# Node sums with the one-hots stationary and the messages in two exact halves, in a graph layer on one Trainium2 core

## The chip, the cores and the metric

One core of a Trainium2 chip runs the whole program. The metric is the device time of one execution in microseconds (us), lower is better. The kernel before takes 1014.85 us, the median of three executions (1013.4 to 1015.24). Engine names: PE is TensorE, ACT ScalarE, DVE VectorE, POOL GpSimd, SP SyncE, which here only issues DMAs.

## What is computed

The layer has three parts over 3125 nodes of 256 numbers and 50000 edges that are sorted by their target. The graph part is the one the change touches:

```
xn  = layernorm(x)
e   = edge_attr @ W_edge + b_edge            # 50000 x 256
msg = relu(xn[src] + e)
agg = segment_sum(msg, dst)                  # 3125 x 256, f32
h   = (1 + eps) * xn + agg
h   = relu(h @ W1 + b1) @ W2 + b2            # then a batch norm over nodes and a relu
x   = x + relu(bn(h)) + linear_attention(xn)
x   = x + mixture_of_experts(layernorm(x))   # 8 experts, top 2, 1024 hidden
```

## The kernel before

All engine programs are written out by hand, with semaphores between them. There are four stages: norms and tables (to about 50 us of the profile), the **edge stage** (to about 560 us), the two-layer MLP with batch norm and the routing (to about 670 us), and the expert blocks (to the end).

The edge stage takes the edges in 66 groups of 768, six tiles of 128 edges each; the last group has one tile. Every engine runs its own loop over n, the number of the group, one group behind the other. For a group:

- SP loads the edge attributes (`load_edges`, L428). POOL gathers the 256 numbers of each edge's source node from a table in HBM, one indirect DMA for each tile of 128 edges (L775), that is 391 in all. They go to a ring of six buffers of two tiles, so POOL may run 12 gathers ahead of DVE's use; each gather reads its row numbers from the table `srcT` in SBUF.
- PE turns the six tiles of attributes (L439), ACT copies them to SBUF (`eaT`, L484), and PE multiplies them by `w_edge` (the embedding, `embed_edges`, L450) into three PSUM banks.
- DVE adds the gathered nodes, pair of tiles by pair (`add_nodes`, L526), into `msg`, and ACT applies the relu in place (`relu_messages`, L498).
- DVE makes the one-hots of the targets inside a window of 128 nodes (`mark_window`, L502, or `mark_from_psum`, L508, which reads its counting row from PSUM). PE multiplies messages and one-hots in full f32 (`aggregate`, L476): the message tile, 128 edges by 128 of the 256 columns, is the stationary operand, the one-hot (128 edges by 128 nodes) the moving one. The sums come out with the columns on the partitions, as the node array `hT` is kept, and DVE adds them to `hT` at the group's window (`add_window`, L544).

Work of other parts rides in the same loops. For n up to 50: keys, values and queries of the attention (PE L924, L932, L941; ACT L1248 to L1250, L1257, L1258; DVE `mix_h` L1571, `mix_k` L1584, `mix_q` L1589). For n from 51: the attention's denominators and outputs (PE L972, L983; ACT L1274, L1280; DVE reciprocals L1604, two for each group, and L1610, one for every two). In every group the expert weights are split in two exact halves for later use: ACT rounds a piece (`round_high`, L581, to the type fp32r), DVE subtracts (`round_low`, L587), SP stores both (L574, L575).

The order in each loop is the order of the code. DVE in iteration n: `mix_h`, `add_window(n - 2)`, the one-hots, `mix_k`, a reciprocal, the three node sums, `mix_q`, `round_low`, a reciprocal and L1610. ACT: the copy of group n + 1's turned attributes, attention work, the three relus of group n, `round_high`. PE: the turn of group n + 1, the embedding of group n, `aggregate(n - 1)`, attention work. After the last group DVE's memset L1697 raises `edges_done`, on which the MLP starts (PE L1040). The input `x`, overwritten by its norm early on, is loaded again into `xs` during n = 51 to 55 (L661), and needed first in front of L1745.

Of the kernel before, what the change touches and what calls it, by code (L numbers as in the profile page):

```python
# [21 lines left out]
F32 = mybir.dt.float32  # L22
# [75 lines left out]
def build(nc, a, out):  # L98
    with ExitStack() as ctx:
# [17 lines left out]
        qT = sb("qT", [P, HALVES, NODES_PAD])  # L117
        xs = sb("xs", [P, TILES, DIM])
# [20 lines left out]
        onehot = view(work, 7680, 2, GT, P)  # L139
# [168 lines left out]
        msg_ready = sem("msg_ready")  # L308
# [150 lines left out]
        def aggregate_tail(pe, n, u):  # L459
            pe.wait_ge(agg_read, n)  # L460
            pe.wait_ge(onehot_ready, n + 1)
            pe.wait_ge(msg_ready, PAIRS * (n + 1))
            for h in range(HALVES):
                last = nc.tensor.matmul(bank[5][:, h * P:(h + 1) * P], msg[:, u, 0, h * P:(h + 1) * P], onehot[:, u, 0],
                                        start=True, stop=True)
            last.then_inc(agg_ready, 1)

        def aggregate(pe, n, u, fresh=False):
# [9 lines left out]
            last.then_inc(agg_ready, 1)  # L478
# [12 lines left out]
        def relu_tail(act, n, u):  # L491
            act.wait_ge(sums_done, PAIRS * (n + 1))
            nc.scalar.activation(msg[:, u, 0], msg[:, u, 0], ACT.Relu).then_inc(msg_ready, PAIRS)
# [27 lines left out]
        def add_nodes(dve, n, u):  # L521
            for q in range(PAIRS):
# [15 lines left out]
        def add_window(dve, n, start, mixed, fresh=False):  # L538
            dve.wait_ge(agg_ready, n + 1)
# [4 lines left out]
            nc.vector.tensor_tensor(w, bank[5][:, 0:DIM].rearrange("p (h c) -> p h c", h=HALVES),  # L544
# [60 lines left out]
        def _(sp):  # L605
# [44 lines left out]
            for n in range(2, GROUPS - 1):  # L650
# [8 lines left out]
                c = n - 2 * TILES - 1  # L659
                if 0 <= c < CHUNKS:  # L660
                    for d, s in node_rows(a["x"], xs[:, c * CHUNK_TILES:(c + 1) * CHUNK_TILES], c):  # L661
                        sp.dma_start(s, d).then_inc(x_again, 16)
# [17 lines left out]
            sp.wait_ge(edges_done, 1)  # L680

# [168 lines left out]
        def _(pe):  # L850
# [140 lines left out]
            for n in range(GROUPS):  # L991
                if n + 1 < GROUPS:
                    transpose_group(n + 1)
                if n < GROUPS - 1:
                    embed_edges(pe, n, n % 2, n == 0)
                else:
                    embed_tail(pe, n, n % 2)
# [5 lines left out]
                if n >= 1:  # L1003
                    aggregate(pe, n - 1, (n - 1) % 2, n == 1)
# [12 lines left out]
            aggregate_tail(pe, GROUPS - 1, (GROUPS - 1) % 2)  # L1017
            again = pe.value_load(miss_i[0:1, 0:1], min_val=0, max_val=1)
            with pe.If(again > 0):
# [5 lines left out]
                with pe.Fori(0, WINDOWS) as w:  # L1025
                    with pe.Fori(0, GROUPS) as g:
# [3 lines left out]
                        aggregate(pe, n, 0)  # L1030
            with pe.Else():
# [169 lines left out]
        def _(act):  # L1201
# [89 lines left out]
            nc.scalar.copy(xw[:], bank[7][0:XROWS, 0:SPLIT * TILE]).then_inc(xw_copied, 1)  # L1291
            for n in range(GROUPS):
                if n + 1 < GROUPS:
                    copy_group(n + 1)
                if 1 <= n <= 2 * TILES:
                    if n % 2 == 1:
                        mix_kv(n // 2)
                    else:
                        mix_q(n // 2 - 1)
                if n == DEN0:  # L1300
# [5 lines left out]
                if n < GROUPS - 1:  # L1306
                    relu_messages(act, n, n % 2)
                else:
                    relu_tail(act, n, n % 2)
# [10 lines left out]
                if n == 6:  # L1320
                    nc.scalar.copy(w2_hi[:], w2[:]).then_inc(w12_high, 1)
            again = act.value_load(miss_i[0:1, 0:1], min_val=0, max_val=1)
            with act.If(again > 0):
                with act.Fori(0, WINDOWS) as w:
                    with act.Fori(0, GROUPS) as g:
                        n = (w + 1) * GROUPS + g
                        copy_edges(act, n, 0, False, 1)
                        relu_messages(act, n, 0)
# [150 lines left out]
        def _(dve):  # L1479
# [140 lines left out]
            for n in range(GROUPS):  # L1620
# [3 lines left out]
                if n >= 2:  # L1624
                    add_window(dve, n - 2, starts[(n - 2) % GT], mixed_by(n + 1), n == 2)
# [9 lines left out]
                if n % 2 == 1 and n < 2 * TILES:  # L1635
                    mix_k(n // 2)
                if n == 2 * TILES:
                    mask_context()
                c, late = (n - DEN0 - 1) // 2, (n - DEN0 - 1) % 2
                if 0 <= c < COL_CHUNKS and not last:  # L1640
                    attn_inverse(c, 2 * late)
                if last:
                    add_tail(dve, n, n % 2)
                else:
                    add_nodes(dve, n, n % 2)
                if n % 2 == 0 and 2 <= n <= 2 * TILES:
# [19 lines left out]
            with dve.If(again > 0):  # L1666
# [16 lines left out]
                with dve.Fori(0, WINDOWS) as w:  # L1683
                    dve.wait_ge(pass_done, w + 1)
                    dve.sem_inc(pass_begun, 1)
                    with dve.Fori(0, GROUPS) as g:
                        n = (w + 1) * GROUPS + g
                        mark_window(dve, g, 0)
                        add_nodes_again(dve, n)
                        add_window(dve, n, w * WINDOW, TILES)  # L1690
# [280 lines left out]
```

## Time and profile before

| | |
|---|---|
| median of three executions | 1014.85 us |
| the profiled execution, its own time | 1009.37 us |
| its span (first to last instruction) | 1007.6 us |
| PE busy | 926.4 us, 92% |
| DVE busy | 601.8 us, 60% |
| POOL busy | 544.6 us, 54% |
| ACT busy | 538.3 us, 53% |
| mean granted TensorE clock | 0.967 of full |

A group row of the profile reads: line, engine, operation, output<-input, shape and count | busy us, mean ns of one | idle us of the engine just before them <- what ended that idle time. "issue" is time in which the engine waited for nothing that the profile shows. In the timeline, each row is the start in us, the duration, the engine, the line, the operation, and in brackets the idle time before it. SBUF tensors that were cut out of larger ones are printed by the larger one's name: `work` holds the messages, one-hots, gathered rows and attributes, `wts` the pieces of weights and `qn`.

### The profile page before, as it was taken

How to read it: one execution, taken by the hardware profiler on the slowest of the kernel's cores; microseconds unless marked ns; L12 is line 12 of the kernel's file. 1: busy time of each engine (PE TensorE's matmuls, PEld its weight loads, DVE VectorE, ACT ScalarE, POOL GpSimd, SP SyncE). 2: the span in 40 equal slices, each digit the busy share in tenths (PEclk: the TensorE clock that was granted, in tenths of full speed). 3: DMA queues.
4: the chain of work that ended last, by engine and by line, in shares of the span. 5: the costliest groups of instructions: out<-in, count | busy, mean ns of one | idle time of the engine just before them, and what ended most of it. 6: DMA issues, size and time to landing. Idle time of an engine off the chain costs nothing.

```text
span 1007.6 us, 17432 instructions
## 1 busy us (share of the span) xinstructions
PE 926.4 (92%) x6055; PEld 824.6 (82%) x6055; DVE 601.8 (60%) x1098; ACT 538.3 (53%) x1064; POOL 544.6 (54%) x527
## 2 busy tenths in 40 slices
PE   5899999999999999999999975379999999999995
PEld 4677889889888888897888765368999999999994
DVE  5555665565665565568989778835554454555442
ACT  2744545445545455445545564836555666555552
POOL 3277777777777777777774004023444444444433
PEclk8899999999999999999999998589999999999998
DMA  9667888877878878799775105459799789888722
GB/s 247 198 165 231 264 259 266 254 253 251 277 243 260 274 252 262 249 304 324 248 241 184 43 1 182 168 201 384 236 312 308 239 289 301 279 253 301 244 42 28
DMA packets 93173, 234.59 MB, mean 233 GB/s; under 512 B 20425, under 2 KB 37843, under 8 KB 84122
## 3 DMA queue, kind: packets, MB, share of 16 engines
q1 hardware_dynamic: 56694, 116.95, 33.9%
q0 software_dynamic: 29136, 64.72, 26.5%
q10 hardware_dynamic: 7252, 51.75, 12.8%
q8 instruction: 52, 0.85, 0.3%
q14 instruction: 39, 0.32, 0.1%
HBM read 183.81 MB, written 50.23 MB: 232 GB/s over the span
## 4 chain that ended last, share of the span: by engine, by line
PE 59%; POOL 13%; DMA 10%; DVE 8%; issue 7%; ACT 2%; DVEq 0%; POOLq 0%; SPq 0%; ACTq 0%
PE banks L1154 15%; POOL work L775 13%; PE banks L1174 10%; DMA work<-node_table,srcT 8%; PE banks L476 7%; PE banks L450 7%; PE banks L1176 5%; PE banks L924 3%; PE banks L983 2%; PE banks L439 2%; PE banks L1063 2%; PE banks L1051 1%; DVE work L526 1%; PE banks L1138 1%; DMA wts<-in_src 1%
## 5 line engine op out<-in xcount | busy, mean ns | idle before, releaser
L775 POOL DMA_INDIRECT work<-node_table,srcT x391 | 382.9, 979 | 151.6 <-issue 109.8
L498 ACT ACTIVATE work<-work 128x512 f32<-128x512 f32 x195 | 120.9, 630 | 127.0 <-DVE work L526 126.3
L476 PEld LDWEIGHTS banks<-work 128*128 128x128 f32 x1560 | 184.2, 192 | 4.5 <-DVE hT L544 1.1
L476 PE MATMUL banks<-work 128*128 128x128 f32 x1560 | 184.8, 275 | 0.7 <-DVE hT L544 0.7
L450 PE MATMUL banks<-w_edge,eaT 128*128 128x256 f32 x780 | 179.1, 379 | 0.0
L526 DVE TENSOR_TENSOR work<-banks,work 128x512 f32<-128x512 f32 x195 | 128.0, 682 | 69.5 <-DMA work<-node_table,srcT 55.1
L824 POOL DMA_INDIRECT out<-work,row_i x54 | 86.5, 1601 | 141.5 <-ACT work L1444 118.9
L1154 PE MATMUL banks<-xe_hi,wup 128*128 128x256 f32 x864 | 158.8, 285 | 3.8 <-DVE xe_lo L1901 3.8
L450 PEld LDWEIGHTS banks<-w_edge,eaT 128*128 128x128 f32 x780 | 143.1, 190 | 17.0 <-issue 0.2
L1174 PE MATMUL banks<-wdown,hid_hi 128*128 x432 | 155.9, 403 | 0.0
L1909 DVE TENSOR_TENSOR hid_lo<-wts,hid_hi 128x512 fp32r<-128x512 f32 x108 | 72.4, 691 | 134.7 <-ACT hid_hi L1421 134.7
L1154 PEld LDWEIGHTS banks<-xe_hi,wup 128*128 128x128 f32 x864 | 136.1, 194 | 5.5 <-DVE xe_lo L1901 4.3
L1154 PE MATMUL banks<-xe_lo,wup 128*128 128x256 f32 x432 | 123.0, 285 | 0.0
L1176 PE MATMUL banks<-wdown,hid_lo 128*128 x432 | 121.3, 281 | 0.0
L484 ACT COPY eaT<-banks 128x768 f32<-128x768 f32 x65 | 51.9, 799 | 115.8 <-PE banks L439 115.7
L814 POOL DMA_INDIRECT work<-token_table,tok_i x54 | 55.6, 1030 | 98.3 <-DVE tok_i L1885 46.8
L1428 ACT ACTIVATE wts<-banks,b1T 128x256 f32<-128x256 f32 x216 | 90.7, 472 | 27.8 <-PE banks L1154 22.6
L1174 PEld LDWEIGHTS banks<-wdown,hid_hi 128*128 128x128 f32 x432 | 81.2, 188 | 18.9
L1154 PEld LDWEIGHTS banks<-xe_lo,wup 128*128 128x128 f32 x432 | 83.8, 194 | 0.0
L1176 PEld LDWEIGHTS banks<-wdown,hid_lo 128*128 128x128 f32 x432 | 81.8, 189 | 0.0
L1421 ACT CAST hid_hi<-wts 128x512 fp32r<-128x512 f32 x108 | 64.1, 621 | 0.0
L439 PEld LDWEIGHTS banks<-ident,work 128*128 128x128 f32 x391 | 46.2, 141 | 21.0 <-issue 18.2
(258 smaller groups left out, 1199.1 us busy)
## 6 DMA issues: line engine op xcount, KB each, us to landing
wup<-split_table ACTq DMA_DIRECT2D x24, 2048.0 KB, 9.7
work<-in_edge_attr SPq DMA_DIRECT2D x65, 384.0 KB, 5.1
wts<-in_L_ffn_W SPq DMA_DIRECT2D x64, 256.0 KB, 4.6
split_table<-raw_hi SPq DMA_DIRECT2D x64, 256.0 KB, 2.6
split_table<-raw_lo SPq DMA_DIRECT2D x64, 256.0 KB, 4.2
wdown<-split_table SPq DMA_DIRECT2D x8, 2048.0 KB, 9.7
work<-node_table,srcT POOLq DMA_INDIRECT x391, 4.5
wup<-split_table SPq DMA_DIRECT2D x3, 2048.0 KB, 8.2
```

Of the source, the lines that this page charges most:

```text
L439: last = nc.tensor.transpose(bank[j // 3][:, (j % 3) * P:(j % 3 + 1) * P], ea[:, u, j], ident[:])
L450: last = nc.tensor.matmul(b[:, k * DIM:(k + 1) * DIM], eaT[:, u, 2 * q + k], w_edge[:], start=True, stop=True)
L476: last = nc.tensor.matmul(bank[5][:, h * P:(h + 1) * P], msg[:, u, j, h * P:(h + 1) * P], onehot[:, u, j], start=(j == 0), stop=(j == GT - 1))
L498: nc.scalar.activation(msg[:, u, 2 * q:2 * q + 2], msg[:, u, 2 * q:2 * q + 2], ACT.Relu).then_inc(msg_ready, 1)
L526: nc.vector.tensor_tensor(msg[:, u, 2 * q:2 * q + 2], bank[2 + q][:].rearrange("p (k c) -> p k c", k=2), xg[i % RING], ALU.add).then_inc(s ...
L775: pool.indirect_dma_start(out=xg[i % RING][0:rows, j % 2], out_offset=None, in_=node_table, in_offset=bass.IndirectOffsetOnAxis(ap=srcT[0: ...
L824: pool.indirect_dma_start(out=out, out_offset=bass.IndirectOffsetOnAxis(ap=row_i[:, i:i + 1], axis=0), in_=ys[:, i % YS], in_offset=None, ...
L1154: last = nc.tensor.matmul(bank[1 + q][:, (c % 2) * BLOCK:(c % 2 + 1) * BLOCK], w[:, s, cols], x[:, u, k], start=(k == 0 and m == 0), stop= ...
L1174: nc.tensor.matmul(b[:].rearrange("p (s c) -> p s c", s=2), hid_hi[:, u, k, cols], w_pair[:, :, k * DIM:(k + 1) * DIM], start=(k == 0), st ...
L1176: last = nc.tensor.matmul(b[:, 0:DIM], hid_lo[:, u, k, cols], w_set[:, k * DIM:(k + 1) * DIM], start=False, stop=(k == HID_CHUNKS - 1), sk ...
L1428: nc.scalar.activation(hid[:, u, c], bank[1 + q][:, (c % 2) * BLOCK:(c % 2 + 1) * BLOCK], ACT.Gelu, bias=b1T[:, bass.ds(e, 1), c]).then_in ...
L1909: nc.vector.tensor_tensor(hid_lo[:, u, 2 * q:2 * q + 2], hid[:, u, 2 * q:2 * q + 2], hid_hi[:, u, 2 * q:2 * q + 2].bitcast(F32), ALU.subtr ...
```

## The change

The one-hot becomes the stationary operand and the message the moving one (256 columns wide), both in fp32r. So that this stays exact, the message is split: ACT's relu writes the rounded high half `msg_hi`, and DVE computes the low half, `msg_lo` = max(msg, 0) - `msg_hi`, over the whole group in one instruction of 1536 elements a partition with two inputs from SBUF. PE accumulates both halves in bank 5: 12 matmuls of 256 columns a group. The sums come out with the nodes on the partitions, so ACT copies them from PSUM to SBUF (`copy_sums`, 256 columns), PE turns them by two transposes (`turn_sums`), and DVE adds these to `hT`.

```
+        def aggregate(pe, n, u, fresh=False, tiles=GT):
             if not fresh:
                 pe.wait_ge(agg_read, n)
             pe.wait_ge(onehot_ready, n + 1)
+            pe.wait_ge(msg_low, n + 1)
+            for j in range(tiles):
+                for m in (msg_hi, msg_lo):
+                    last = nc.tensor.matmul(bank[5][:, 0:DIM], onehot[:, u, j], m[:, u, j],
+                                            start=(j == 0 and m is msg_hi), stop=(j == tiles - 1 and m is msg_lo))
+            last.then_inc(agg_ready, 1)
+
+        def turn_sums(pe, n):
+            pe.wait_ge(sums_copied, n + 1)
             for h in range(HALVES):
-                for j in range(GT):
-                    if h == 0 and j % 2 == 0:
-                        pe.wait_ge(msg_ready, PAIRS * n + j // 2 + 1)
-                    last = nc.tensor.matmul(bank[5][:, h * P:(h + 1) * P], msg[:, u, j, h * P:(h + 1) * P], onehot[:, u, j],
-                                            start=(j == 0), stop=(j == GT - 1))
-            last.then_inc(agg_ready, 1)
+                last = nc.tensor.transpose(bank[5][:, DIM + h * P:DIM + (h + 1) * P], sums[:, h * P:(h + 1) * P], ident[:])
+            last.then_inc(turned, 1)
...
+        def copy_sums(act, n):
+            act.wait_ge(agg_ready, n + 1)
+            nc.scalar.copy(sums, bank[5][:, 0:DIM]).then_inc(sums_copied, 1)
...
-        def relu_messages(act, n, u):
+        def high_messages(act, n, u):
             for q in range(PAIRS):
                 act.wait_ge(sums_done, PAIRS * n + q + 1)
-                nc.scalar.activation(msg[:, u, 2 * q:2 * q + 2], msg[:, u, 2 * q:2 * q + 2], ACT.Relu
-                                     ).then_inc(msg_ready, 1)
+                nc.scalar.activation(msg_hi[:, u, 2 * q:2 * q + 2], msg[:, u, 2 * q:2 * q + 2], ACT.Relu
+                                     ).then_inc(msg_high, 1)
+
+        def low_messages(dve, n, u, tiles=GT):
+            dve.wait_ge(msg_high, PAIRS * (n + 1))
+            nc.vector.scalar_tensor_tensor(out=msg_lo[:, u, 0:tiles], in0=msg[:, u, 0:tiles], scalar=0.0,
+                                           in1=msg_hi[:, u, 0:tiles].bitcast(F32), op0=ALU.max, op1=ALU.subtract
+                                           ).then_inc(msg_low, 1)
...
         def add_window(dve, n, start, mixed, fresh=False):
-            dve.wait_ge(agg_ready, n + 1)
+            dve.wait_ge(turned, n + 1)
```

`msg_hi` and `sums` take the place of `xs`, which is free during the stage once the tables are made, so ACT waits for `rows_ready` ahead of its loop, and the second load of `x` moves from n = 51 to 55 to behind `edges_done`:

```
             sp.wait_ge(edges_done, 1)
+            for c in range(CHUNKS):
+                for d, s in node_rows(a["x"], xs[:, c * CHUNK_TILES:(c + 1) * CHUNK_TILES], c):
+                    sp.dma_start(s, d).then_inc(x_again, 16)
```

The loops change their order (unchanged lines between are left out):

```
 PE      for n in range(GROUPS):
             transpose_group(n + 1)
+            if n >= 2:
+                turn_sums(pe, n - 2)
             embed_edges(pe, n, n % 2, n == 0)
-            if n >= 1:
-                aggregate(pe, n - 1, (n - 1) % 2, n == 1)
             mix_kv / mix_q, mix_context / attn_den
+            if n >= 1:
+                aggregate(pe, n - 1, (n - 1) % 2, n == 1)
             attn_out
+        turn_sums(pe, GROUPS - 2)
+        aggregate(pe, GROUPS - 1, (GROUPS - 1) % 2, tiles=1)
+        turn_sums(pe, GROUPS - 1)

 ACT     for n in range(GROUPS):
-            copy_group(n + 1)
+            if n >= 2:
+                copy_sums(act, n - 2)
             mix_kv / mix_q
+            copy_group(n + 1)
             copy_attn_w, attn_den, attn_bias
-            relu_messages(act, n, n % 2)
+            high_messages(act, n, n % 2)
             round_high(act, n - 2)

 DVE     for n in range(GROUPS):
             h_group(n + 1)
             if n >= 2:
-                add_window(dve, n - 2, starts[(n - 2) % GT], mixed_by(n + 1), n == 2)
+                dve.wait_ge(agg_ready, n - 1)
             mark_window / mark_from_psum, mix_k
+            mix_q(n // 2 - 1)
+            if n >= 2:
+                add_window(dve, n - 2, starts[(n - 2) % GT], mixed_by(n + 1), n == 2)
             attn_inverse(c, 2 * late)
             add_nodes of all three pairs
-            mix_q(n // 2 - 1)
             round_low(dve, n - 3)
+            low_messages(dve, n, n % 2, 1 if last else GT)
             attn_inverse(c, 2 * late + 1), attn_norm(c)
```

## Rows read from the trace of the kernel before

**Rows 1.** Windows of the edge stage and the MLP: busy us of each engine (count), PEclk, DMA share, GB/s.

```profile
100.00:447.00 347.00, 342.13 (x2282) 303.45 (x2281) 204.67 (x342) 176.46 (x341) 264.07 (x273) 1.00 0.82 261
447.00:557.00 110.00, 107.73 (x641) 88.47 (x639) 94.58 (x116) 55.97 (x95) 75.26 (x75) 1.00 0.79 247
557.00:600.00 43.00, 39.20 (x180) 33.12 (x179) 32.96 (x56) 24.92 (x37) 0.00 (x0) 1.00 0.05 20
```

**Rows 2.** Groups by line over the whole run: the gathers.

```profile
L775 POOL DMA_INDIRECT work<-node_table,srcT x391 | 382.9, 979 | 151.6 <-issue 109.8 <-DMA node_table<-work 32.7 <-DVE work L526 9.1
```

**Rows 3.** The gathers by line L775: durations, and time from issue to landing.

```profile
L775 POOL DMA_INDIRECT work<-node_table,srcT x391: 918/949/1857, 43.0 to 543.9; - x196
...
DMA to landing us min/median/max: 2.7/4.5/7.6
```

**Rows 4.** Timeline of DVE: `add_window` of groups 4 and 50, 46 groups apart.

```profile
96.45 0.42 DVE L544 TENSOR_TENSOR hT<-banks,hT 128x256 f32 x1 [0.26 <-PE banks L476]
...
448.30 0.42 DVE L544 TENSOR_TENSOR hT<-banks,hT 128x256 f32 x1
```

**Rows 5.** Chain of waits, start and us: the embedding and the sums of a group, and the next embedding.

```profile
348.50 2.59 PE banks L450 x12
351.10 2.68 PE banks L476 x24
355.77 2.59 PE banks L450 x12
```

**Rows 6.** Timeline of DVE and POOL, three pieces: gathers that start during a DVE instruction.

```profile
431.26 0.69 DVE L587 TENSOR_TENSOR raw_lo<-wts,raw_hi 128x512 fp32r<-128x512 f32 x1 [1.28 <-ACT raw_hi L581]
431.33 1.44 POOL L775 DMA_INDIRECT work<-node_table,srcT  x1 [0.30 <-issue]
...
463.69 1.54 DVE L1604 RECIPROCAL wts<-wts 128x224 f32<-128x224 f32 x1
464.07 0.94 POOL L775 DMA_INDIRECT work<-node_table,srcT  x1 [0.30 <-issue]
465.27 1.09 DVE L1610 SCALAR_TENSOR_TENSOR wts<-wts,qT 128x896 f32<-128x896 f32 x1
465.31 1.86 POOL L775 DMA_INDIRECT work<-node_table,srcT  x1 [0.30 <-issue]
...
132.79 0.75 DVE L587 TENSOR_TENSOR raw_lo<-wts,raw_hi 128x512 fp32r<-128x512 f32 x1
132.81 0.95 POOL L775 DMA_INDIRECT work<-node_table,srcT  x1 [0.30 <-DVE work L526]
```

**Rows 7.** Chain of waits: 48 matmuls of 256 columns in fp32r, in an expert block.

```profile
730.45 5.76 PE banks L1154 x48
```

**Rows 8.** Timeline of PE: the turn of a group, six transposes.

```profile
308.93 0.82 PE L439 MATMUL banks<-ident,work 128*128 128x128 f32 x6
```

**Rows 9.** Groups of ACT between 100 and 557 us: a copy of 256 columns from PSUM.

```profile
L1250 ACT COPY v_t<-banks 125x256 f32<-125x256 f32 x22 | 8.5, 388 | 0.0
```

**Rows 10.** Groups of DVE between 100 and 557 us, by shape.

```profile
L587 DVE TENSOR_TENSOR raw_lo<-wts,raw_hi 128x512 fp32r<-128x512 f32 x60 | 41.2, 687 | 19.4 <-ACT raw_hi L581 9.9 <-issue 9.5
L1610 DVE SCALAR_TENSOR_TENSOR wts<-wts,qT 128x896 f32<-128x896 f32 x6 | 6.6, 1092 | 0.2
```

**Rows 11.** Timeline of DVE: from behind the last node sums of group 64 to the stage's end.

```profile
550.30 0.68 DVE L587 TENSOR_TENSOR raw_lo<-wts,raw_hi 128x512 fp32r<-128x512 f32 x1
...
559.63 0.27 DVE L1697 MEMSET eq<- 128x250 f32 x1
```

**Rows 12.** PE at L924 behind a gap, a window around it, and L924 without a gap.

```profile
86.72 3.54 PE L924 MATMUL banks<-wkvT,qT 128*125 128x512 f32 x4 [2.14 <-DVE qT L1589]
...
84.00:91.00 7.00, 4.86 (x17) 2.53 (x16) 3.50 (x6) 1.66 (x3) 5.48 (x6) 0.76 0.71 217
...
299.95 1.88 PE L924 MATMUL banks<-wkvT,qT 128*125 128x512 f32 x4
```

More of the change, by code:

```diff
@@ L117, in build @@
         qT = sb("qT", [P, HALVES, NODES_PAD])
+        xs_offset = next_offset()
         xs = sb("xs", [P, TILES, DIM])
@@ L138, in build @@
         msg = view(work, 4608, 2, GT, DIM)
-        onehot = view(work, 7680, 2, GT, P)
+        msg_lo = nc.alloc_sbuf_tensor_at("msg_lo", [P, 2, GT, DIM], F32R, offset=work_offset + 4 * 4608)
+        msg_hi = nc.alloc_sbuf_tensor_at("msg_hi", [P, 2, GT, DIM], F32R, offset=xs_offset)
+        sums = xs[:, 12]
+        onehot = nc.alloc_sbuf_tensor_at("onehot", [P, 2, GT, P], F32R, offset=work_offset + 4 * 7680)
         table_stage = view(work, 1536, STAGES * CHUNK_TILES, DIM).rearrange("p (u t) d -> p u t d", u=STAGES)
@@ L307, in build @@
         sums_done = sem("sums_done")
-        msg_ready = sem("msg_ready")
+        msg_high = sem("msg_high")
+        msg_low = sem("msg_low")
+        sums_copied = sem("sums_copied")
+        turned = sem("turned")
         onehot_ready = sem("onehot_ready")
@@ L457, in embed_tail @@
             nc.tensor.matmul(bank[2][:, 0:DIM], eaT[:, u, 0], w_edge[:], start=True, stop=True).then_inc(e_ready, PAIRS)
[L459 to L465, printed above, removed]
-            last.then_inc(agg_ready, 1)
-        def aggregate(pe, n, u, fresh=False):
+        def aggregate(pe, n, u, fresh=False, tiles=GT):
             if not fresh:
@@ L519, in add_tail, with add_nodes @@
             nc.vector.tensor_tensor(msg[:, u, 0], bank[2][:, 0:DIM], xg[i % RING][:, 0], ALU.add).then_inc(sums_done, PAIRS)
-        def add_nodes(dve, n, u):
-            for q in range(PAIRS):
+        def add_nodes(dve, n, u, pairs=range(PAIRS)):
+            for q in pairs:
                 i = PAIRS * n + q
@@ L543, in add_window @@
             w = hT[:, :, bass.ds(start, WINDOW)]
-            nc.vector.tensor_tensor(w, bank[5][:, 0:DIM].rearrange("p (h c) -> p h c", h=HALVES),
+            nc.vector.tensor_tensor(w, bank[5][:, DIM:2 * DIM].rearrange("p (h c) -> p h c", h=HALVES),
                                     w, ALU.add).then_inc(agg_read, 1)
@@ L658, in _ @@
                     load_raw(sp, n - 3)
[L659 to L662, printed above, removed]
             load_tail(sp, GROUPS - 1, 1)
@@ L1030, in _ @@
                         aggregate(pe, n, 0)
+                        turn_sums(pe, n)
             with pe.Else():
@@ L1291, in _ @@
             nc.scalar.copy(xw[:], bank[7][0:XROWS, 0:SPLIT * TILE]).then_inc(xw_copied, 1)
+            act.wait_ge(rows_ready, CHUNKS)
             for n in range(GROUPS):
-                if n + 1 < GROUPS:
-                    copy_group(n + 1)
+                if n >= 2:
+                    copy_sums(act, n - 2)
                 if 1 <= n <= 2 * TILES:
@@ L1321, in _ @@
                     nc.scalar.copy(w2_hi[:], w2[:]).then_inc(w12_high, 1)
+            for n in range(GROUPS - 2, GROUPS):
+                copy_sums(act, n)
             again = act.value_load(miss_i[0:1, 0:1], min_val=0, max_val=1)
@@ L1327, in _ @@
                         copy_edges(act, n, 0, False, 1)
-                        relu_messages(act, n, 0)
+                        high_messages(act, n, 0)
+                        copy_sums(act, n)
             with act.Else():
@@ L1641, in _ @@
                     attn_inverse(c, 2 * late)
+                if not last:
+                    add_nodes(dve, n, n % 2, range(PAIRS - 1))
                 if last:
@@ L1644, in _ @@
                 else:
-                    add_nodes(dve, n, n % 2)
-                if n % 2 == 0 and 2 <= n <= 2 * TILES:
-                    mix_q(n // 2 - 1)
+                    add_nodes(dve, n, n % 2, (PAIRS - 1,))
                 if n >= 1 and (n - 1) % GT == 0:
@@ L1689, in _ @@
                         add_nodes_again(dve, n)
+                        low_messages(dve, n, 0)
                         add_window(dve, n, w * WINDOW, TILES)
```

10 lines of the change are left out of this document (5 added, 5 removed).

## The prediction, made before the changed kernel ran

> **What bounds the kernel now.** I read the page first: PE is busy 92% of the span and looks like the bound of every stage. In the edge stage that is only half of it. The windows [rows 1] show PE busy 342 of 347 us for n below 51, but POOL's 264 is not its real occupation: each gather takes 0.95 us [rows 3] and has 0.30 of "issue" in front (109.8 us, and 9.1 put down to DVE: together 0.305 for each of 390) [rows 2]. So a gather costs 1.25 us and six make 7.50. From the start of the first to that of the last 500.9 us pass [rows 3], where 390 x 1.25 are 488: in the whole stage POOL stands still for 13 us only. A group took (448.30 - 96.45)/46 = 7.65 us [rows 4], POOL's pace. PE's pace is much the same: two embeddings in a row start 7.27 us apart [rows 5], and it is busy 98.6% of its time. **POOL's issuing of gathers is the bound to n = 50, with PE level with it**; behind that the attention work makes PE the slower one, busy 107.7 of 110 us [rows 1], in which 13 full groups and a short one of some 3 us pass, so 8.2 a group against POOL's 7.5, paid out of POOL's lead of 12 gathers.
>
> The 13 us matter most. Where a gather starts while DVE runs an instruction whose two inputs both lie in SBUF, it lasts until about 0.8 us behind DVE's end: 1.44 us beside L587 and 1.86 us beside L1610, instead of 0.95; beside the reciprocal, with one input, it took 0.94 [rows 6]. Over the gathers from 49 us on, 39 are longer than usual by over 0.05 us, and each has L587, L1610, L1571, L502 or a split of w1 or w2 over its start, all with two SBUF inputs; only four starts under such an instruction went free, one of them in the third piece of [rows 6]. The delay is DVE's end less 0.12 us less the gather's start (431.95 - 0.12 - 431.33 = 0.50, seen 0.49; 466.36 - 0.12 - 465.31 = 0.93, seen 0.91).
>
> **The change, part by part.**
>
> *PE.* Removed: 24 half-matmuls of f32, 2.68 us a group [rows 5]. Added: 12 fp32r matmuls of 256 columns at 5.76/48 = 0.12 us [rows 7], 1.44 us, and two transposes at 0.82/6 = 0.137 us [rows 8], 0.27. PE saves 0.97 us a group, 63 us of its own time in the stage. On the clock this brings nothing to n = 50, as POOL holds the pace at 7.5 or more; PE's work goes from 342/347 x 7.65 = 7.5 [rows 1] to 6.5 us a group.
>
> *ACT.* The relus and `round_high` stay in number and size; the relus now write fp32r, as `round_high` does. `copy_sums` adds 0.39 us [rows 9]: ACT was busy 176 of 347 us [rows 1], so 3.9 of 7.65 us a group, now 4.3. It is first in each iteration, behind `high_messages` and `round_high` of the group before; PE's `turn_sums(n - 2)`, with the embedding of n queued behind it, therefore waits for DVE's last sum of n - 1, then relu, rounding, copy and semaphores, some 2.2 us. From there PE has 6.5 us to do and must be there again a group later: it fits in 8.6 us, with about 2 us idle. The wait for `rows_ready` is in front of the loop, where DVE's tables are done before POOL's first gather (which waits for their stores): nothing.
>
> *DVE.* `low_messages` is 1536 elements with two inputs in SBUF. From 512 elements at 687 ns and 896 at 1092 [rows 10] an element costs 1.055 ns: 687 + 1024 x 1.055 = 1.77 us, 65 times with the short last one apart. To n = 50 DVE was busy 205/347 x 7.65 = 4.5 us a group, now 6.3: still under POOL's pace, and its wait for ACT's last high half is mostly under `round_low`. `mix_q` now stands ahead of the sums and `add_window` behind it, where it waits for PE's turn with the node sums queued behind; the turn is there some 2.5 us after the last sum of the group before, while DVE still has low half and one-hots to do, so neither costs anything. In the attention part it was busy 94.6 us [rows 1] for 13 full groups and a short one, about 7.0 each; now 7.0 + 1.77 + 0.1 of waiting = 8.9 against 8.2 before. There DVE becomes a bound.
>
> *POOL, the term that decides.* 1.77 us is longer than the 1.25 us between gathers, so every `low_messages` covers at least one start. If the next start comes u after its own, the delay is 1.77 - 0.12 - u, between 0.40 (u = 1.25) and 1.65 (u = 0). What sets u is a landing, and landings come 2.7 to 7.6 us after the issue [rows 3], more than a period apart, so I take u evenly spread: 1.65 - 0.625 = 1.02 us, for the 64 groups whose low half comes while gathers are still issued: 65 us. `round_low` sits directly in front, and today holds up a start by 0.57 x 0.57/2/1.25 = 0.13 us on average; a gather just held up is not held again, so I take those 8 us off: **+57**. POOL has nothing to pay this from: it is the bound.
>
> The Trainium skill speaks to this in "SBUF — State Buffer", section "Who interferes with whom": tensor_tensor with both inputs in SBUF contends with GpSimd's reads, yet a probe saw it not stall DMA, since writing descriptors needs only the write interface (which the page calls inferred). Read so, the low half would cost POOL nothing and the sum would lose its 57 us. The trace disagrees: L587 is a tensor_tensor, and gathers beside it took up to 0.5 us longer.
>
> *Attention part and tail.* POOL now needs 7.5 + 0.4 (today's delays there) + 0.9 = 8.8 us a group, DVE 8.9, and the small difference and unlucky orders add about **+3**. At the end, from L587 of group 64 to the memset are 9.3 us today [rows 11]; behind the last sums now stand the low half (1.77), the copy (0.39) and the turn (0.27) with three more semaphores, less the shorter matmuls: **+3**.
>
> *SP.* The ten loads of `x` (3.2 MB) leave n = 51 to 55 and are issued behind `edges_done`. They are needed about 41 us later, in front of L1745; the queues moved 261 GB/s in the stage and stand nearly still in the MLP, 20 GB/s [rows 1], so 3.2 MB take about 12 to 20 us there: hidden. Were the cover gone, it would cost those 20 us at most. No other DMA is added or passed.
>
> Sum against the profiled execution: 1009.4 + 57 + 3 + 3 = 1072. The median lies 5.5 us above that execution, so 1077 us. All behind `edges_done` stays as it is.
>
> **Bounds.** POOL's delay: 0.40 a group gives 26 less 8 = +18; 1.65 gives +98. Phases that lock, because landing, sum and low half follow the gather by a nearly fixed time, could favour either end.
>
> **The rivals.**
>
> *Low halves do not hold POOL up.* To n = 50 nothing changes; behind it DVE is the bound with 8.9 against 8.2 us, 13 groups, +9, tail +3: 1027 us. For it speak the four starts that went free, all within 0.08 us of DVE's own start; 39 against four speak against it. Chance 0.10. This is what the Trainium skill's sentence on the probe would give.
>
> *Faster than before.* PE is what really paces the stage (its chain rows are unbroken for many groups), and the low half slips between gathers. Place: n = 51 to 65, where PE loses 0.97 us of its 8.2 a group. It decides from the point at which DVE's work there stays under 8.2 us, that is a low half under 1.1 us. POOL's floor of 488 us caps the gain at 13 us, to about 1003. Against it: no DVE row with 1536 elements could be that short, and POOL's rows show no slack. Chance 0.04.
>
> *PE's clock falls.* PE would be busy 6.5 of 8.6 us with gaps near 2 us. Behind a gap of 2.14 us L924 took 3.54 us where it takes 1.88, and the granted clock around it was 0.76 [rows 12]: part of that stretch ran at 1.2 GHz instead of 2.4. Were this so in every group, PE would need 6.5 + 1.7 = 8.2 us and stand level with POOL; with the wait on ACT the loop could grow by some 0.5 us a group, +33: 1110 us. A gap that shrinks for it removes its own cause, so chance 0.08.
>
> *The change does not do what it says* (for instance matmuls at f32's pace): PE would then be at 9 us a group, 65 x 0.5 more: also near 1110. The fp32r row makes it unlikely: 0.02.
>
> The main forecast has 0.76; its range by itself is 1045 to 1105. Of that 0.76 about 0.70 lies inside, the clock's 0.08 and the 0.02 beside it are at the upper edge, and the first rival stays mostly out; so the whole range is 1036 to 1110, which reaches toward that rival without taking it in. A measurement here tells about 0.2% (2 us) from no change; faster is the second rival, 0.04; same, 0.02, is the thin end of the first; slower is the rest, 0.94.
>
> **What would show it.** Right: the gathers' mean goes from 979 ns to about 1120, with one per group at 1.4 to 2.6 us over the start of the STT of 1536 elements (1.77 us each), the last gather near 600 us, PE busy about 63 us less in the stage and idle once a group at the transposes of `sums`; DVE's waits on landings stay. `edges_done` near 622 us and 448 us behind it as before. Wrong: gathers still at 0.95 beside the low half (first rival); a granted clock under 0.95 in the edge stage (third); groups longer than 9 us with POOL waiting for DVE's sums would mean a loop through ACT and PE that I held for slack.

## The result, and the profile after

The changed kernel takes 1064.97 us (median of 4, 1062.82 to 1067.85) against 1014.12 us: ratio 1.0506, 95% interval 1.0473 to 1.0539. It is slower by 51 us. The profiled execution took 1066.0 us with a span of 1064.3 us, 56.7 us more than the one of before, which lay 5 us under its own median.

Windows of the kernel after, as in [rows 1] (busy us of PE, PE's loads, DVE, ACT and POOL, then granted clock, DMA share, GB/s): to n = 50, the attention part, the tail of the edge stage, the MLP's start.

```profile
100.00:487.00 387.00, 318.35 (x1848) 264.21 (x1848) 281.47 (x396) 188.77 (x394) 303.51 (x275) 0.97 0.73 235
487.00:606.00 119.00, 97.42 (x478) 73.92 (x476) 112.40 (x123) 56.59 (x104) 81.26 (x76) 0.96 0.64 205
606.00:613.00 7.00, 3.06 (x18) 2.18 (x18) 3.90 (x9) 1.68 (x4) 0.00 (x0) 0.97 0.20 75
613.00:630.00 17.00, 16.65 (x59) 12.44 (x60) 13.38 (x20) 8.75 (x13) 0.00 (x0) 0.81 0.82 220
```

PE, busy 98.6% of its time before [rows 1], is now busy 82%, and the stage is longer all the same. The group rows of the gathers and of the low half, which answer to [rows 2] and [rows 10]:

```profile
L787 POOL DMA_INDIRECT work<-node_table,srcT x391 | 429.0, 1097 | 154.0 <-issue 106.3 <-DMA node_table<-work 33.0 <-DVE work L539 14.7
L510 DVE SCALAR_TENSOR_TENSOR msg_lo<-work,msg_hi 128x1536 fp32r<-128x1536 f32 x66 | 114.7, 1738 | 8.7 <-issue 2.1 <-ACT msg_hi L505 1.4
```

The gathers' busy time went from 382.9 to 429.0 us, 46.1 more, while their median is 946 ns, against 949 before: 104 of the 391 are longer than 0.995 us, where 40 were, and the rest are as before.

```profile
L787 POOL DMA_INDIRECT work<-node_table,srcT x391: 909/946/2527, 43.3 to 592.4; - x196
...
DMA to landing us min/median/max: 2.7/3.5/7.7
```

The timeline shows one such case, from `round_low` (L600) on:

```profile
234.40 0.68 DVE L600 TENSOR_TENSOR raw_lo<-wts,raw_hi 128x512 fp32r<-128x512 f32 x1
234.89 1.01 POOL L787 DMA_INDIRECT work<-node_table,srcT  x1 [0.30 <-issue]
235.18 1.76 DVE L510 SCALAR_TENSOR_TENSOR msg_lo<-work,msg_hi 128x1536 fp32r<-128x1536 f32 x1
...
235.98 0.44 PE L480 MATMUL banks<-ident,xs 128*128 128x128 f32 x2 [2.78 <-ACT xs L496]
236.21 1.55 POOL L787 DMA_INDIRECT work<-node_table,srcT  x1 [0.30 <-issue]
236.25 4.44 PE L457 MATMUL banks<-w_edge,eaT 128*128 128x256 f32 x12
```

A gather starts at 234.89 during `round_low`, is let go as that ends (1.01 us), and 1.32 us after its start the next comes, 1.03 us into the low half (L510, to 236.94). It takes 1.55 us: 236.94 - 0.12 - 236.21 = 0.61 over the usual 0.945. Over the stage, 63 gathers are held up in this way by the low half, 51 us in all, 0.81 each; all gathers together lie 60 us over 391 x 0.945, before 13. PE meanwhile idles 2.78 us at `turn_sums` (L480), waiting for ACT's copy, and runs the embedding behind it slower: its twelve half-matmuls take 4.44 us, where the timeline of before has 2.76 for a group (2.59 in the chain of [rows 5]). That is one of the slowest; of the 47 embeddings between 100 and 487 us whose twelve records are all in the trace, four took 4.44 us or more. The granted clock of the stage fell from 1.00 to 0.97.

The pace, by `add_window` of groups 4, 50 and 63, which answers to [rows 4], and one more row of the kernel before, of group 63:

```profile
102.46 0.42 DVE L557 TENSOR_TENSOR hT<-banks,hT 128x256 f32 x1
...
487.09 0.42 DVE L557 TENSOR_TENSOR hT<-banks,hT 128x256 f32 x1
...
606.73 0.42 DVE L557 TENSOR_TENSOR hT<-banks,hT 128x256 f32 x1
```

```profile
552.37 0.36 DVE L544 TENSOR_TENSOR hT<-banks,hT 128x256 f32 x1
```

Groups 4 to 50: 8.36 us each (384.6/46) against 7.65. Groups 50 to 63: 9.20 us (119.6/13) against 8.01 (104.1/13). By these rows the kernel after is 6.0 us late at group 4, 32.8 us more by group 50 and 15.6 us more by group 63. Part of the first 6 us is only that `add_window` now stands further back in DVE's loop. The stage's end, which answers to [rows 11]:

```profile
592.43 0.91 POOL L787 DMA_INDIRECT work<-node_table,srcT  x1 [0.32 <-DVE work L539]
...
593.27 0.68 DVE L600 TENSOR_TENSOR raw_lo<-wts,raw_hi 128x512 fp32r<-128x512 f32 x1
...
613.03 0.27 DVE L1726 MEMSET eq<- 128x250 f32 x1
```

The last gather ends 48.5 us later than before, `edges_done` 53.4 us later (613.03 against 559.63). The last 3.3 us came behind it (451.3 us to the end of the span against 448.0; in the versions of the changed kernel below that run the same expert blocks it was 449.2 to 450.9): PE was busy 3.06 of 7 us in the tail, and the clock in the MLP's first 17 us was 0.81, against 1.00 [rows 1].

### The profile page after: what moved, and what is told of

It reads as the page before. It is cut to its first block, busy times and chain, and to the rows that moved or that the text cites. A ratio compares the mean times of both kernels' runs of the same rounds, so it can differ in the third digit from the quotient of the medians.

```text
span 1064.3 us, 16313 instructions
## 1 busy us (share of the span) xinstructions
PE 889.1 (84%) x5405; PEld 767.0 (72%) x5405; DVE 705.7 (66%) x1164; ACT 552.2 (52%) x1130; POOL 591.1 (56%) x527
## 3 DMA queue, kind: packets, MB, share of 16 engines
q1 hardware_dynamic: 56694, 116.95, 32.1%
## 4 chain that ended last, share of the span: by engine, by line
PE 38%; POOL 18%; DVE 14%; DMA 12%; issue 12%; ACT 3%; DVEq 1%; POOLq 0%; SPq 0%; ACTq 0%
POOL work L787 18%; PE banks L1171 15%; DMA work<-node_table,srcT 10%; PE banks L1191 10%; PE banks L1193 5%; DVE work L539 3%; ACT msg_hi L505 2%; PE banks L1080 2%; DVE wts L1627 2%; PE banks L1068 1%; PE banks L1155 1%; DVEq L1638 1%; PE banks L995 1%; DMA wts<-in_src 1%; DVE hT L557 1%
## 5 line engine op out<-in xcount | busy, mean ns | idle before, releaser
L787 POOL DMA_INDIRECT work<-node_table,srcT x391 | 429.0, 1097 | 154.0 <-issue 106.3
L505 ACT ACTIVATE msg_hi<-work 128x512 fp32r<-128x512 f32 x195 | 120.6, 631 | 271.8 <-DVE work L539 271.3
L457 PE MATMUL banks<-w_edge,eaT 128*128 128x256 f32 x780 | 190.7, 397 | 0.0
L457 PEld LDWEIGHTS banks<-w_edge,eaT 128*128 128x128 f32 x780 | 151.2, 201 | 19.9
L473 PE MATMUL banks<-msg_hi,onehot 128*128 128x256 f32 x391 | 114.0, 327 | 13.1 <-DVE hT L557 13.1
L510 DVE SCALAR_TENSOR_TENSOR msg_lo<-work,msg_hi 128x1536 fp32r<-128x1536 f32 x66 | 114.7, 1738 | 8.7 <-issue 2.1
L473 PE MATMUL banks<-msg_lo,onehot 128*128 128x256 f32 x391 | 98.3, 287 | 0.0
L473 PEld LDWEIGHTS banks<-msg_hi,onehot 128*128 128x128 f32 x391 | 76.0, 194 | 23.6 <-DVE hT L557 16.2
L480 PE MATMUL banks<-ident,xs 128*128 128x128 f32 x132 | 28.9, 301 | 74.1 <-ACT xs L496 74.1
```

The source lines that it names most:

```text
L457: last = nc.tensor.matmul(b[:, k * DIM:(k + 1) * DIM], eaT[:, u, 2 * q + k], w_edge[:], start=True, stop=True)
L473: last = nc.tensor.matmul(bank[5][:, 0:DIM], onehot[:, u, j], m[:, u, j], start=(j == 0 and m is msg_hi), stop=(j == tiles - 1 and m is ms ...
L505: nc.scalar.activation(msg_hi[:, u, 2 * q:2 * q + 2], msg[:, u, 2 * q:2 * q + 2], ACT.Relu).then_inc(msg_high, 1)
L510: nc.vector.scalar_tensor_tensor(out=msg_lo[:, u, 0:tiles], in0=msg[:, u, 0:tiles], scalar=0.0, in1=msg_hi[:, u, 0:tiles].bitcast(F32), op ...
L787: pool.indirect_dma_start(out=xg[i % RING][0:rows, j % 2], out_offset=None, in_=node_table, in_offset=bass.IndirectOffsetOnAxis(ap=srcT[0: ...
```

## The experiments

Each was timed beside the kernel before on the same chip. The stage's end is read from the memset that raises `edges_done`, in the rows with its start time ("576.7 to 576.7").

**The low half with one SBUF input.** Same instruction, same length, but the second input is the counting row in PSUM, for groups 3 to 49:

```
+        def low_from_counting(dve, n, u):
+            ...
+            nc.vector.scalar_tensor_tensor(out=msg_lo[:, u]..., in0=msg[:, u]..., scalar=0.0,
+                                           in1=numbers.unsqueeze(1).to_broadcast([P, 2 * GT, P]), op0=ALU.max, op1=ALU.subtract
```

> The changed kernel, but for groups 3 to 49 the subtraction in the low half takes as its second input a counting row in PSUM (broadcast to 1536 elements) in place of the high half in SBUF. So the low half's value is not computed there; the number of instructions, their length and order stay. Theory (two inputs from SBUF hold up the start of a gather): the 63 long gathers of the changed kernel (51 us over the usual 0.945 us) fall to some 16, the gathers' busy time falls by about 38 us, and the kernel takes 1065 - 38 = about 1027 us. Rival (DVE's extra 1.75 us a group, or the loop through ACT's copy and PE's turn, sets the pace): nothing changes, 1065 us.

```profile
L795 POOL DMA_INDIRECT work<-node_table,srcT x391 | 390.2, 998 | 155.2 <-issue 105.7 <-DMA node_table<-work 32.9 <-DVE work L547 16.6
L517 DVE SCALAR_TENSOR_TENSOR msg_lo<-work,banks 128x1536 fp32r<-128x1536 f32 x47 | 82.4, 1753 | 3.8
L844 POOL DMA_INDIRECT out<-work,row_i x64 | 105.4, 1647 | 186.6 <-DMA out<-work,row_i 116.7 <-ACT work L1475 60.7 <-issue 9.1
L1737 DVE MEMSET eq<- x1: 267/267/267, 576.7 to 576.7; 128x250 f32 x1
```

Its `add_window` rows of groups 50 and 63:

```profile
453.21 0.42 DVE L565 TENSOR_TENSOR hT<-banks,hT 128x256 f32 x1
...
569.15 0.42 DVE L565 TENSOR_TENSOR hT<-banks,hT 128x256 f32 x1
```

The instruction took 1753 ns, as with two SBUF inputs, and the gathers' busy time fell to 390.2 us, by 38.8. The stage ended at 576.7 us instead of 613.0, 36.3 us earlier, and groups 4 to 50 had 7.66 us each, the pace of the kernel before. DVE, ACT and PE had the same instructions in the same order; only where one operand lay was changed, and DVE waits first for the counting row, which cost it next to nothing (3.8 us of idle time in front of all 47). The low halves of the first three groups and from n = 50 on are still those with two SBUF inputs: 16 of them held up a gather, 10.5 us in all, 13 of these behind n = 49. The total, 1104.95 us (ratio 1.0895, 1.0868 to 1.0922), missed my 1027, and tells nothing on this: without the low half's value the routing sends the tokens elsewhere, and the branch with five further expert blocks runs, as its 64 stores show where 54 are usual, two a block. I had not thought of that when I wrote the number.

**One idle instruction in the kernel before**, with two SBUF inputs or with one; nothing else of the change:

```
                 if n >= 3:
                     round_low(dve, n - 3)
+                if 3 <= n <= 46:
+                    dve.wait_ge(mx_ctx, (n + 1) // 2)
+                    ...
+                    nc.vector.scalar_tensor_tensor(out=xs[0:TILE, 0:GT]..., in0=xs[0:TILE, GT:2 * GT]..., scalar=0.0,
+                                                   in1=<xs[0:TILE, 2 * GT:3 * GT], or numbers broadcast>, ...)
```

> The kernel before, with one idle instruction more on DVE behind round_low in groups 3 to 46 (44 of them): 1536 elements, both inputs from SBUF, like the low half; it reads and writes the part of xs that nobody uses then, and nobody waits for it. Nothing else of the change is in it. Theory: each holds up one gather by 0.8 to 1.0 us, so 35 to 45 us more: 1050 to 1059 us, gathers' busy time up by the same. Rival (the change costs its time through PE's and ACT's new order, not through POOL): DVE has room, 4.5 of 7.65 us a group, so under 3 us more.

> As the run with the idle instruction of two SBUF inputs, but its second input is the counting row in PSUM. Theory: same DVE time, no gather held up: within 3 us of the kernel before, 1012 to 1017 us. Rival (DVE's time itself costs): the same 35 to 45 us as with two SBUF inputs.

With two SBUF inputs:

```profile
L776 POOL DMA_INDIRECT work<-node_table,srcT x391 | 415.0, 1061 | 151.6 <-issue 111.5 <-DMA node_table<-work 32.7 <-DVE work L527 7.3
L1657 DVE SCALAR_TENSOR_TENSOR xs<-xs 125x1536 f32<-125x1536 f32 x44 | 77.1, 1752 | 16.6 <-PE banks L942 16.5
L1706 DVE MEMSET eq<- x1: 267/267/267, 593.0 to 593.0; 128x250 f32 x1
```

With the second one in PSUM:

```profile
L776 POOL DMA_INDIRECT work<-node_table,srcT x391 | 381.7, 976 | 155.7 <-issue 109.7 <-DMA node_table<-work 32.9 <-DVE work L527 13.1
L1657 DVE SCALAR_TENSOR_TENSOR xs<-xs,banks 125x1536 f32<-125x1536 f32 x44 | 76.9, 1748 | 25.9 <-PE banks L942 25.6
L1706 DVE MEMSET eq<- x1: 267/267/267, 563.9 to 563.9; 128x250 f32 x1
```

The two instructions take the same 1.75 us of DVE. The first costs 34 us (1047.89 us, ratio 1.0343, 1.0313 to 1.0373), the second nothing that can be measured (1013.35 us, ratio 0.9986, 0.9969 to 1.0003). The gathers' busy time is 32.1 us more in the first, 0.73 for each of 44 instructions, and 1.2 less in the second. That is just under the 35 to 45 us and the 1050 to 1059 us that I expected for the first. Each of the 44 held up one gather, by 0.81 us on average. To n = 50, DVE's time costs nothing and PE's new order is not needed for the loss: the operand's place is the cause.

**PE's saving taken back.** In the changed kernel every matmul of the sums is done twice:

```
+            for j in range(tiles):
+                for m in (msg_hi, msg_lo):
+                    nc.tensor.matmul(bank[5][:, 0:DIM], onehot[:, u, j], m[:, u, j], start=True, stop=True)
             for j in range(tiles):
```

> The changed kernel with PE's saving taken back: each group's 12 matmuls of the sums are done twice, once into the bank with no use and then as they should, 12 x 0.12 = 1.44 us a group more on PE, so 8 us instead of 6.5 for n below 51. Theory (POOL and, in the attention part, DVE set the pace): PE's idle time shrinks, the kernel takes 1065 to 1073 us. Rival (PE's order with its turn behind ACT's copy sets the pace): 65 x 1.44 = up to 94 us more, 1159 us; half of that would mean that PE is level with POOL.

```profile
L790 POOL DMA_INDIRECT work<-node_table,srcT x391 | 428.1, 1095 | 157.1 <-issue 105.1 <-DMA node_table<-work 32.8 <-DVE work L542 19.1
L1729 DVE MEMSET eq<- x1: 267/267/267, 616.8 to 616.8; 128x250 f32 x1
```

1071.41 us (ratio 1.0556, 1.0526 to 1.0586): 65 x 1.44 = 94 us of matmuls more cost 6 us. PE does not set the pace; its saving was worth next to nothing where it was made. The gathers' row is that of the changed kernel. The granted clock from 100 to 487 us was 1.00 here, and groups 4 to 50 took 8.43 us each, no less than the 8.36 at 0.97.

**The low half pair by pair**, three instructions of 512 elements, two of them between the node sums:

```
                 if not last:
                     add_nodes(dve, n, n % 2, range(PAIRS - 1))
+                    low_pair(dve, n, n % 2, 0)
                 ...
                     add_nodes(dve, n, n % 2, (PAIRS - 1,))
+                    low_pair(dve, n, n % 2, 1)
                 ...
-                low_messages(dve, n, n % 2, 1 if last else GT)
+                    low_pair(dve, n, n % 2, PAIRS - 1)
```

> The changed kernel, computing the same, but the low half is made pair by pair: three instructions of 512 elements (0.69 us each, like round_low), the first two behind the second and the third node sum, the last behind round_low. DVE's time grows by some 0.2 us a group. Theory: a short instruction holds up the next gather only if that starts within its first 0.57 us, 0.13 us on average, so three cost 0.4 us a group instead of 0.8: 25 us less, and some 4 us back in the attention part where DVE is full: about 1043 us (1036 to 1055). Rival (DVE's time is what costs): 1065 to 1078 us.

```profile
L798 POOL DMA_INDIRECT work<-node_table,srcT x391 | 395.8, 1012 | 160.3 <-issue 106.0 <-DMA node_table<-work 33.0 <-DVE work L550 21.3
L520 DVE SCALAR_TENSOR_TENSOR msg_lo<-work,msg_hi 128x512 fp32r<-128x512 f32 x195 | 133.7, 686 | 9.2 <-ACT msg_hi L505 2.2 <-issue 1.5
L1742 DVE MEMSET eq<- x1: 267/267/267, 586.4 to 586.4; 128x250 f32 x1
```

1039.25 us (ratio 1.0243, 1.0204 to 1.0281), 26 us less than the changed kernel, although DVE spends 133.7 us on it instead of 114.7. The gathers' busy time fell by 33 us: the low halves' own hold-ups went from 51.0 to 11.6 us (39 gathers), those beside other instructions rose from 8.5 to 14.7. The attention part got slower, 9.29 us a group instead of 9.20; DVE was busy 38.1 of 40 us there (520 to 560 us), against 37.0.

**The node sums kept in PSUM.** The same result as the changed kernel; the low half reads PSUM and `msg_hi`:

```
-                nc.vector.tensor_tensor(msg[:, u, 2 * q:2 * q + 2],
+                nc.vector.tensor_tensor(bank[2 + q][:].rearrange("p (k c) -> p k c", k=2),
...
-            nc.vector.scalar_tensor_tensor(out=msg_lo[:, u, 0:tiles], in0=msg[:, u, 0:tiles], scalar=0.0,
+            nc.vector.scalar_tensor_tensor(out=msg_lo[:, u, 0:tiles],
+                                           in0=banks[:, 1024:1024 + tiles * DIM].rearrange("p (j c) -> p j c", c=DIM), scalar=0.0,
...
-                if not fresh:
-                    pe.wait_ge(sums_done, PAIRS * (n - 1) + q + 1)
+                if not fresh and q == 0:
+                    pe.wait_ge(msg_low, n)
```

> The changed kernel, computing the same, but DVE writes the node sums back into their PSUM banks instead of SBUF, ACT's relu reads them there, and the low half reads PSUM and the high half, so has one SBUF input only. Price: PE's next embedding has to wait for the low half, since its banks are free only then. Theory: the low halves' hold-ups (51 us) go; what is left over the kernel before is the attention part, where DVE needs 8.9 us a group against 8.2, and the longer tail: 1018 to 1030 us. If the wait of the embedding for the low half closes a loop longer than POOL's 7.5 us: up to 1050 us with gathers at 0.95 us and POOL waiting for sums. Rival (hold-ups are not the cause): 1065 us or more.

```profile
L788 POOL DMA_INDIRECT work<-node_table,srcT x391 | 386.4, 988 | 159.0 <-issue 103.0 <-DMA node_table<-work 33.0 <-DVE banks L540 23.1
L510 DVE SCALAR_TENSOR_TENSOR msg_lo<-banks,msg_hi 128x1536 fp32r<-128x1536 f32 x65 | 114.1, 1756 | 9.0 <-ACT msg_hi L505 3.0 <-issue 2.1
L457 PE MATMUL banks<-w_edge,eaT 128*128 128x256 f32 x780 | 203.3, 416 | 38.2 <-DVE msg_lo L510 37.9
L1727 DVE MEMSET eq<- x1: 267/267/267, 576.8 to 576.8; 128x250 f32 x1
```

1025.37 us (ratio 1.0112, 1.0088 to 1.0137), in the range of the theory, and 40 us under the changed kernel with the same DVE time for the low half. No low half held up a gather. The embedding does wait for it (37.9 us in all), at a place where PE has room: groups 4 to 50 take 7.72 us, and that at a granted clock of 0.95, lower than the 0.97 of the changed kernel. The profiled stage ends 17.1 us later than that of the kernel before; 11.7 of them lie in the attention part, 8.90 us a group, where a window shows DVE busy 39.5 of 40 us and POOL no longer at its pace (25 gathers in 40 us, where 32 would fit):

```profile
520.00:560.00 40.00, 33.14 (x167) 24.71 (x166) 39.52 (x43) 20.53 (x39) 25.60 (x25) 1.00 0.60 187
100.00:480.00 380.00, 341.49 (x1937) 286.08 (x1936) 306.51 (x417) 199.09 (x413) 290.02 (x296) 0.95 0.80 254
```

**DVE's time in the attention part by itself.** The kernel before with one idle reciprocal, one SBUF input, in groups 52 to 64:

```
+                if 52 <= n <= 64:
+                    ...
+                    nc.vector.reciprocal(early[:, 0:2 * P]..., ones[:].unsqueeze(1).to_broadcast([P, 2, P]))
```

> The kernel before, with one idle reciprocal of 256 elements (one input from SBUF, by the row of 224 elements about 1.77 us) behind round_low in groups 52 to 64, that is in the attention part alone; nobody waits for it, and nothing else is changed. Theory (DVE becomes the bound there, apart from any hold-up): a group takes 8.9 instead of 8.01 us, the stage ends 12 us later, 1026 us. Rival (the lead of the gathers and PE's larger work cover it, and the whole cost of the change is POOL's): under 4 us more, 1014 to 1018 us.

```profile
L776 POOL DMA_INDIRECT work<-node_table,srcT x391 | 387.1, 990 | 157.1 <-issue 107.2 <-DMA node_table<-work 32.6 <-DVE work L527 17.2
L1703 DVE MEMSET eq<- x1: 267/267/267, 573.1 to 573.1; 128x250 f32 x1
```

Its `add_window` rows of groups 50 and 63:

```profile
450.67 0.42 DVE L545 TENSOR_TENSOR hT<-banks,hT 128x256 f32 x1
...
567.22 0.36 DVE L545 TENSOR_TENSOR hT<-banks,hT 128x256 f32 x1
```

1021.94 us (ratio 1.0070, 1.0042 to 1.0098): 8.6 us by the medians, between the rival's 4 and my 12. A group takes 8.97 us there (116.55/13), near the forecast. By the profiles the stage ends 13.5 us later, but the profile of before is one of the faster executions, and 2.4 of the 13.5 are there at group 50, ahead of the first reciprocal added. So 1.75 us a group on DVE, which cost nothing to n = 50, cost about 1 us a group in the attention part (8.97 against 8.01). It was not hold-ups: gathers that started between the two rows lie 6.7 us over their usual time, against 5.2 in the kernel before.

**What sets the size of a hold-up.** In the changed kernel `round_low` moves ahead of the node sums:

```
+                if n >= 3:
+                    round_low(dve, n - 3)
                 if not last:
                     add_nodes(dve, n, n % 2, range(PAIRS - 1))
                 ...
-                if n >= 3:
-                    round_low(dve, n - 3)
                 low_messages(dve, n, n % 2, 1 if last else GT)
```

> The changed kernel, computing the same, but round_low (two inputs from SBUF, 0.69 us) stands in front of the three node sums instead of directly in front of the low half. In the changed kernel 42 of 63 gathers that the low half holds up start 1.02 to 1.04 us behind the low half's start and are held up by 0.61 us; 20 start within 0.55 us and are held up by 1.1 to 1.6 us. Theory: round_low sets this phase, since a gather that comes during it is let go at its end, and the next then comes 1.03 us into the low half. Without it in front the phase is even: 1.0 us instead of 0.81 for each low half, and round_low's own delays come on top: 10 to 15 us more, 1075 to 1080 us, and the heap at 1.03 us gone. Rival (the phase comes from the landings and ACT's relu, round_low has no part in it): heap and time stay, 1065 us.

```profile
L787 POOL DMA_INDIRECT work<-node_table,srcT x391 | 439.8, 1125 | 157.5 <-issue 110.6 <-DMA node_table<-work 33.0 <-DVE work L539 13.9
L510 DVE SCALAR_TENSOR_TENSOR msg_lo<-work,msg_hi 128x1536 fp32r<-128x1536 f32 x65 | 114.3, 1759 | 61.3 <-ACT msg_hi L505 38.3 <-issue 23.0
L1726 DVE MEMSET eq<- x1: 267/267/267, 627.9 to 627.9; 128x250 f32 x1
```

1078.77 us (ratio 1.0639, 1.0611 to 1.0668), 14 us more. The expectation counted the heap too high: in the changed kernel 31 of the 63 gathers start 1.02 to 1.03 us behind the low half, 12 more at 1.07 to 1.28 us and 20 within 0.9 us. Of the 43 late ones, 35 come right behind a gather that `round_low` had held up. In this run the heap is gone: four of 63 start at 1.00 to 1.05 us, the others are spread from 0.10 to 1.25, and the mean hold-up rose from 0.81 to 0.99 us, 62 instead of 51 us. So `round_low` made the heap. All gathers together lost 10.8 us more; the rest of the 14 us is another matter: the low half now waits for ACT's last relu in the open (38.3 us in all), which counts in the attention part, 9.56 us a group.

## Why the prediction was right, and where it was off

The direction, the cause and the range held: 1065 us in 1036 to 1110, 12 us under the 1077.

- **POOL is the bound to n = 50.** Shown: doubling PE's matmuls of the sums cost 6 us, 1.75 us more of DVE without a second SBUF input cost nothing, and what the gathers gained when the hold-ups went the stage's end gained too (38.8 and 36.3 us).
- **The low half holds up one gather a group.** Shown from both sides, by taking the second SBUF input out of the changed kernel and by putting it into the one before. The formula, DVE's end less 0.12 us less the start, held for all 63 to 0.01 us; the low half failed to hold the gather at its start twice, each within 0.04 us of its own start. In the trace of before the prediction counted four such free starts; there are six, at 0.00 to 0.08 us, which changes nothing in the argument.
- **Its size, the term that was mis-sized.** I put +57, 65 for the low halves less 8 for `round_low`; the gathers' time grew by 46.1, 51.0 for the low halves less 4.9 for all others. The step that failed is "so I take u evenly spread". It was not: 31 of 63 starts came at 1.02 to 1.03 us, with a hold-up of 0.61 us, and 12 later still, near the mild end of 0.40 to 1.65. `round_low` stands directly in front with two SBUF inputs, so it collects the gathers that come during its 0.69 us and lets them go at its end, and the next start is then 1.03 us into the low half. I had taken `round_low` in only as 8 us saved, and those did not come: gathers beside it lost 7.4 us, where they had lost 6.6. What fell were the hold-ups beside the one-hots, `mix_h` and L1610, from 5.1 to 0.7 us. With `round_low` moved away u was even, and the mean 0.99 us, near the 1.02 of the sum.
- **The attention part, put in the wrong account.** I charged hold-ups for all 64 groups, so 11.6 us for the last 13, and +3 for DVE on top. These 13 groups took 15.6 us more, 9.20 us a group against 8.01, and 0.9 of the 1.2 us are DVE's own time: without any hold-up by a low half a group takes 8.90 us (sums in PSUM), and 8.97 with only an idle instruction on DVE. It also took 8.92 (115.94/13) in the run with the counting row, although 13 low halves of this part held up gathers there. So in that run these hold-ups cost nothing that shows in the pace. What makes it 9.20 in the changed kernel was not tried; DVE stood idle 6.6 us between the two rows, against 3.0 with the sums in PSUM. For the stage's end this gives three shares: 36.3 of the 53.4 us go with the hold-ups of groups 3 to 49, and about 12 (13 x 0.9) are DVE's in the attention part, which would come without any. In the run with the counting row the other 5 us are there at group 50 already (453.2 against 448.3). No run takes them apart, and they are no more than profiles differ: with the idle instruction that reads PSUM, which cost nothing by the medians, the stage also ended 4.3 us later (563.9) than in the fast profile of before.
- **Tail and behind.** From the end of the last gather to `edges_done` 19.7 us instead of 14.8: +4.9 where I had +3. Behind `edges_done` I had nothing and 3.3 us came, with a lower clock after PE's idle tail. The other versions with this tail have 1.2 to 2.9 us there, so the size is uncertain. The loads of `x` moved there run beside it, 220 GB/s in that window; what part of the 3.3 us is theirs was not tried.
- **The offset.** I added 5.5 us because the profiled execution lay under the median. The one after lies 1 us over its own. So 6.5 of the 12 us come from there, which is luck of the profiled executions, and about 6 from the sum, which said 63 us above the profiled 1009.4 where 56.6 came.
- **First rival** (no hold-ups, 1027 us): it did not happen, but its price was right. The version whose low halves hold nothing up takes 1025 us. The sentence of the Trainium skill, "SBUF — State Buffer", section "Who interferes with whom", that a tensor_tensor was not seen to stall DMA does not hold for these gathers: beside L600, a tensor_tensor, 33 were longer, by 0.22 us on average, and beside the low half, a scalar_tensor_tensor, up to 1.6 us. Its other rule, that a DVE instruction with two SBUF inputs contends with a GpSimd instruction that reads SBUF, is what the runs agree with, 1047.9 against 1013.4 us for two equally long instructions.
- **Clock rival.** The clock did fall, to 0.97, and an embedding behind a gap at `turn_sums` took 4.44 us instead of 2.76. It did not set the pace: with the sums in PSUM the clock was lower, 0.95, and a group took 7.72 us; with the matmuls doubled it was 1.00, and a group took 8.43.

No version beat the kernel before. The saving of 63 us was on an engine that had another one level with it, and what POOL needed beyond 390 x 1.25 us in the whole stage was 13 us. These 13 us were not idle time either, as the prediction has it, but hold-ups: the gathers of before lie 13.4 us over 391 x 0.945.

## What to carry to other kernels

Before an engine is relieved, add up what the next one needs including its "issue" gaps: POOL looked 76% busy here and was full. Here 63 of 65 low halves, 1.76 us long with two SBUF inputs, held up the indirect DMA that POOL started meanwhile. One input in PSUM took the hold-ups away, at the same length, and pieces of 0.69 us, shorter than the 1.25 us between two gathers, won back 26 of the 51 us by which the changed kernel was slower. What 1.75 us more on DVE cost apart from that depended on the place: nothing where DVE had room, 0.9 to 1.0 us in the attention part, where DVE had been busy 86% of the time [rows 1] and was now full. How long a hold-up was depended on what ran directly in front.

## What was not expected

- A short instruction with two SBUF inputs directly in front of a long one lowers the long one's hold-up from 0.99 to 0.81 us on average, since it sets the phase of the gathers. Moving it away, with no work added, cost 14 us, of which the gathers' time is 10.8.
- DVE took the same for 1536 elements with both inputs in SBUF (1752 ns), with 1536 elements of one input in PSUM (1756 ns) and with 12 repeats of a PSUM row as one input (1748 and 1753 ns).
- A gather that is already under way hardly disturbs DVE: 49 low halves of the changed kernel began up to 0.9 us behind a gather's start, and they took 1.75 to 1.76 us like the others.
